# A residual added on TensorE as two rounded parts, and a bias moved from the values to the residual

## The chip, the cores and the metric

One core of one Trainium2 chip runs the whole program. The metric is the device time of one execution in microseconds (us). A core has five engines that run side by side, each with its own queue of instructions in program order: TensorE (PE; its weight loads are shown as PEld), VectorE (DVE), ScalarE (ACT), GpSimd (POOL) and SyncE (SP). They wait for each other by semaphores alone.

## The reference

x is 16 sequences of 56 tokens of 128 features. First a cross attention by autocorrelation, then a mixture of 8 experts, both added to x with a tanh gate:

```python
Q, K, V = norm(x) @ Wq + bq, ctx[:, :56] @ Wk + bk, ctx[:, :56] @ Wv + bv   # 16 heads of 8
corr = irfft(rfft(Q) * conj(rfft(K))).mean(over the 8 of a head)
w, idx = top_k(corr, 4); w = softmax(w)
out = sum_k w[k] * roll(V, -idx[k])                                        # per head
x = x + tanh(g_xattn) * (out @ Wo + bo)
logits = norm(x) @ Wr + br; weights = softmax over the 2 largest of 8
h = gelu(norm(x) @ W1[e] + b1[e]); y_e = h @ W2[e] + b2[e]                 # 128 -> 512 -> 128
x = x + tanh(g_ffn) * sum_e weights[e] * y_e
```

The weights w of a head sum to one. So the bias bv of the values comes out of the attention as bv @ Wo for every token.

## The kernel before, in words

The tokens lie in 8 tiles of 112 (two sequences each). Tiles 0 to 3 are half 0, 4 to 7 half 1, and each half has two quarters (q = 0, 1) of two tiles. `f(half, q)` in the code and in this text is the step f for that quarter. Every engine's order is written out by hand: a function for each step, waits inside it, and the calls below each other at the end of the engine's block.

The front (the attention) goes through these steps, most of them on TensorE with a copy by another engine behind each:

- keep_busy (L918): FILLERS products of a zero tile with 512 columns, before any data is there.
- context_spectra, x_spectra: discrete Fourier transform along the sequence, as a product with a table; for x on the normalised tiles xn. The results are copied to cf and xf.
- open_projection (L922) adds a bias row as a product with one row of contraction, keys, queries and values (L949, L955, L960) are the products with the weights.
- times_keys and scores on VectorE multiply the spectra, head_sums (L969) sums over a head, correlations (L981) goes back to lags, replaced and kept on VectorE find the 4 largest, exponentials on ScalarE, weights_turned (L987), weight_spectra (L991), own_columns on VectorE (L690), repeated (L997), weighted and output_spectra on VectorE (tw and of).
- output_products (L1007): of times Wo, copied with the gate to y_sb (gated, L480). add_residual (L1017) writes the residual into PSUM bank q as an f32 product with an identity of 112, and attention (L1022) adds the way back from the spectrum on top.
- xres is made on GpSimd (residual, L352): x plus the gated bias bo, in four instructions. It waits for shared (L365), which waits for the gate's tanh of ScalarE (L525).
- attended_moments and the following on VectorE, invert(1, half) on GpSimd (L336: one over the square root of the variances) and shifts(1, half) on VectorE (L620) give the second norm. VectorE and ScalarE make the normalised tiles xn, tokens_turned (L1055) transposes them into PSUM, and ScalarE and VectorE make of it a rounded lead xth (L493) and a rest xtl (L721). attended on ScalarE (L485) copies the attention's result from PSUM to x2.

The experts: all large products are made from fp32r (rounded) operands. A value is kept as a lead (rounded) and a rest (what rounding left), and a product is the sum of lead times lead, rest times lead and lead times rest. hidden(n, halves) (L1073) makes chunk n of 128 hidden features (4 chunks for each of 8 experts), ScalarE applies gelu and makes its lead, VectorE the rest (L735), project(n, halves) (L1097) is the second product. Both go over 448 tokens (a half) at a time. The weights' lead is made by ScalarE (lead, L459) for experts 0 and 1 and by GpSimd for the others, the rest by GpSimd (rest, L343, in pieces of 128 columns for experts 0 to 2, L408 whole for the others).

GpSimd's order in the front is: invert(0,0), invert(0,1), shared, residual four times, rest(0,0), rest(0,1), rest(1,0), invert(1,0), rest(1,1), lead(2,0), one piece of rest(2,0), invert(1,1), and on. Each of its instructions on this path waits for the one before it to be finished.

PSUM has 8 banks. hidden writes bank 2 * (n % 2) + half, so chunk 0 of half 0 writes bank 0, where attention(1,0) had put its result; `if n == 0 and halves == A: pe.wait_ge(x2_ok, 3)` holds it until that is copied.

Of the kernel before, what the change touches and what calls it, by code (L numbers as in the profile page):

```python
# [25 lines left out]

FILLERS = 10
SLOTS = 3
# [25 lines left out]
B_EVEN = B_ID + D  # L54
TAB_B = B_EVEN + 2

P_B2, P_B1, P_WR = 0, E, E + E * HC
# [30 lines left out]
def build(nc, first, second, w_attn, bias_rows, gates, shared_rows, cols, w_experts, tab_b, tab_c, out, route_dram):  # L88
    with ExitStack() as stack:
# [9 lines left out]
        back = sb("back", [PT, 2, HT, D])  # L99
        tb = sb("tb", [D, TAB_B])  # L100
        tc = sb("tc", [D, HT + 1, D])
        wa_sb = sb("wa_sb", [D, 4, D])
        rows_sb = sb("rows_sb", [1, 3, D])
        shared = sb("shared", [PT, D + E])
# [6 lines left out]
        tanh_g = sb("tanh_g", [D, 2])  # L111
        xres = sb("xres", [PT, NT, D])
        minus_half = sb("minus_half", [PT, HT])
        stat = sb("stat", [PT, NT, 6])
# [68 lines left out]
        c_spec, cf_ok = sem("context_spectra"), sem("context_spectra_in_sbuf")  # L183
        x_spec, xf_ok = sem("x_spectra"), sem("x_spectra_in_sbuf")
        k_proj, v_proj, q_proj = sem("k_projected"), sem("v_projected"), sem("q_projected")
# [8 lines left out]
        y_mm, y_ok, attn, x2_ok = sem("y_products"), sem("y_in_sbuf"), sem("attention_out"), sem("x2_ready")  # L194
        tanh_ok, xres_ok = sem("gates_ready"), sem("residual_with_bias")
        xt_mm, xth_ok, xt_ok = sem("x2_transposed"), sem("x2_lead"), sem("x2_split")
        wrc_mm, wrc_ok = sem("router_centred"), sem("router_centred_in_sbuf")
# [43 lines left out]
        def nth(half, q):  # L241

            return 2 * half + q + 1
# [39 lines left out]
        def banks_of(n, halves):  # L283

            return slice(2 * (n % 2) + halves[0], 2 * (n % 2) + halves[-1] + 1)

# [41 lines left out]
        def _(gp):  # L328
# [19 lines left out]
            def residual(half, q):  # L348
# [5 lines left out]
                gp.wait_ge(xres_ok, nth(half, q))  # L354

            def lead(e, k):

                gp.tensor_copy(weh[:, e, k, :], we_sb[:, e % RING, k, :]).then_inc(lead_p, 1)  # L358
                gp.wait_ge(lead_p, 2 * (e - LEAD_BY_SCALAR) + k + 1)
# [5 lines left out]
            gp.tensor_scalar(shared[:, 0:D], shared[:, 0:D], tanh_g[0:PT, 0:1], None, ALU.mult).then_inc(pool, 1)  # L365
            gp.wait_ge(pool, 1)
            residual(0, 0)
            residual(0, 1)
            residual(1, 0)
            residual(1, 1)  # L370
            gp.wait_ge(in_we[0], 16)
            gp.wait_ge(lead_s, 1)
            rest(0, 0)
            gp.wait_ge(lead_s, 2)
            rest(0, 1)
            gp.wait_ge(in_we[1], 16)
            gp.wait_ge(lead_s, 3)
# [38 lines left out]
        def _(act):  # L416
# [21 lines left out]
            def x_spectra(half, q):  # L438
                act.wait_ge(x_spec, nth(half, q))
                act.copy(xf[:, half, q * QS:(q + 1) * QS], bank[:, 2 + q, 0:QS]).then_inc(xf_ok, 1)  # L440

# [73 lines left out]
            take(kf, 0, 4)  # L515
            x_spectra(0, 0)
            x_spectra(0, 1)
            take_swapped(kf, 0, 4, 1)
            take_negated(kf, 0, 4, 1, k_ok)
            context_spectra(1)  # L520
            normalise(tokens, 0, 6)
            normalise(tokens, 0, 4)
            lead(0, 0)
            act.wait_ge(in_g, 16)
            act.activation(tanh_g[:, :], g_sb[:, :], ACT.Tanh).then_inc(tanh_ok, 1)  # L525
            act.wait_ge(k_proj, 2)
# [5 lines left out]
            exponentials(0)  # L532
            take_negated(kf, 1, 5, 1, k_ok)
            act.wait_ge(v_proj, 1)
            take(vf, 0, 0)
            lead(1, 0)
            weights_turned(0)
            take_swapped(vf, 0, 0, 0)
            act.wait_ge(v_proj, 2)
# [3 lines left out]
            take_negated(vf, 1, 1, 0, v_ok)  # L543
            head_sums(1)
            gated(0, 0)
            exponentials(1)
            gated(0, 1)
            act.wait_ge(wrc_mm, 1)
# [36 lines left out]
        def _(ve):  # L585
# [46 lines left out]
            def columns(q):  # L632
                return slice(q * QS, (q + 1) * QS)

            def times_keys(half, q):
# [150 lines left out]
            def take_expert(e, half):  # L786

                ve.wait_ge(y_expert, product_of(HC * e + HC - 1, half))
                if e >= 2:
# [5 lines left out]
                                        op0=ALU.add, op1=ALU.mult).then_inc(scaled_ok, 1)  # L795

            def turned_routes():
                ve.wait_ge(route_mm, 1)
                ve.tensor_copy(route_t[:, :], bank[0:E * NT, 5, 0:PT]).then_inc(route_sb, 1)
# [22 lines left out]
            measured_b = aggregates(second_half, measured_b)  # L822
            variances(1, measured_b)
            times_keys(0, 0)
            shifts(0, 1)
# [3 lines left out]
            normalise(tokens, 5)  # L829
            normalise(tokens, 7)  # L830
            head_sums(0)
            replaced(0)
# [81 lines left out]
        def _(pe):  # L914
# [37 lines left out]
            def queries(half, q):  # L952
                pe.wait_ge(xf_ok, nth(half, q))
                into = bank[:, 6, q * QS:(q + 1) * QS] if half else bank[:, 6 + q, 0:QS]
                pe.matmul(into, wa_sb[:, 0, :], xf[:, half, q * QS:(q + 1) * QS], start=False, stop=True,  # L955
                          skip_group_check=True).then_inc(q_proj, 1)

            def values(half):
                open_projection(2, half, HT)
                pe.matmul(bank[:, half, 0:HS], wa_sb[:, 2, :], cf[:, half, :], start=False, stop=True,  # L960
                          skip_group_check=True).then_inc(v_proj, 1)

# [48 lines left out]
            def add_residual(half, q):  # L1011

                if nth(half, q) == 1:
                    pe.wait_ge(xres_ok, 4)
                if not half:
                    pe.wait_ge(v_ok, q + 1)
                pe.matmul(bank[0:PT, q, 0:QT * D], ident[0:PT, 0:PT],  # L1017
                          xres[:, quarter(half, q), :].rearrange("p i d -> p (i d)"), start=True, stop=False)

# [38 lines left out]
            def hidden(n, halves):  # L1058
# [4 lines left out]
                if n >= 2:  # L1063
                    pe.wait_ge(gelu_ok, unit(n - 2, halves[-1]))
                if n == 0 and halves == A:
                    pe.wait_ge(x2_ok, 3)
                cols_ = slice(c * D, (c + 1) * D)
                operands = ((weh, xth), (wel, xth), (weh, xtl))
                for k, (w, t) in enumerate(operands):
                    for half in halves:  # L1070
                        if n == 0:
                            pe.wait_ge(xt_ok if k == 2 else xth_ok, half + 1)
                        mm = pe.matmul(bank[:, 2 * (n % 2) + half, 0:TOK], w[:, e, 0, cols_], t[:, half, :],  # L1073
                                       start=(k == 0), stop=(k == 2))
# [38 lines left out]
            x_spectra(0, 1)  # L1113
            context_spectra(1)
            queries(0, 0)
            queries(0, 1)
            pe.wait_ge(in_wvo, 16)
            values(0)
            keys(1)
            pe.wait_ge(in_tb, 16)  # L1120
            head_sums(0, 0)
# [3 lines left out]
            x_spectra(1, 1)  # L1125
            pe.wait_ge(qk_mul, 1)
            open_projection(0, 6, HT)
# [108 lines left out]
```

## Time and profile before

| | us |
|---|---|
| median of 3 runs | 117.72 (117.53 to 117.83) |
| the profiled execution | 117.55 |
| its span, first to last instruction | 115.7 |
| busy: TensorE, its weight loads | 110.0, 93.8 |
| busy: VectorE, ScalarE, GpSimd | 85.1, 81.6, 73.1 |

The span leaves 1.85 us around it. All durations in this text are of the one profiled execution. A matmul's duration in a timeline holds the way through the array, so rows that follow each other overlap; the chain of waits counts each stretch of time once. An f32 product shows as two matmuls, an fp32r product as one.

### The profile page before, as it was taken

To read this page: it belongs to the slowest core of one execution; us is meant where nothing else is said; L and a number is where in the kernel's file an instruction comes from. 1 tells how busy PE (TensorE), PEld (TensorE's weight loads), DVE (VectorE), ACT (ScalarE), POOL (GpSimd) and SP (SyncE) were. 2 spreads that over 40 slices of the span, in tenths; PEclk is the share of its full clock that TensorE was granted. 3 is DMA by queue.
4 is the path that set the end of the run, shared out by engine and by line. 5 is a ranking of instruction groups with operands and counts; after the bars stand their busy time and mean duration, and the time that the engine had idled before them with its cause. 6 is when DMAs were issued, how large, how long until landed. Compare 5 with 4: busy or idle time off the path is not lost.

```text
span 115.7 us, 1754 instructions
## 1 busy us (share of the span) xinstructions
PE 110.0 (95%) x577; PEld 93.8 (81%) x577; DVE 85.1 (74%) x174; ACT 81.6 (70%) x120; POOL 73.1 (63%) x74
## 2 busy tenths in 40 slices
PE   6999999999899999999999999999999999999960
PEld 2488778668578898999899999999999999999950
DVE  0473577878679998586987499769789746878891
ACT  0447986359489669978878868888778887788900
POOL 1123498813898603999999999999999702405500
PEclk9999999999999999999999999999999999999998
DMA  3989300130050050298084000400300300000004
GB/s 80 271 275 417 151 0 6 51 133 0 0 181 3 7 180 0 50 289 330 5 340 135 25 0 9 150 0 3 157 1 6 136 22 0 0 0 0 3 0 159
DMA packets 4223, 10.34 MB, mean 89 GB/s; under 512 B 837, under 2 KB 1590, under 8 KB 4214
## 3 DMA queue, kind: packets, MB, share of 16 engines
q1 hardware_dynamic: 3442, 9.65, 24.1%
q10 hardware_dynamic: 772, 0.59, 1.9%
q8 instruction: 4, 0.07, 0.2%
q14 instruction: 5, 0.04, 0.1%
HBM read 9.75 MB, written 0.49 MB: 88 GB/s over the span
## 4 chain that ended last, share of the span: by engine, by line
PE 88%; ACT 4%; DVE 3%; POOL 2%; issue 1%; DVEq 0%; POOLq 0%
PE bank L1073 34%; PE bank L1097 33%; PE bank L918 4%; PE bank L943 2%; PE bank L960 2%; PE bank L922 2%; POOL wel L343 2%; PE bank L934 2%; PE bank L955 2%; PE bank L949 2%; PE bank L969 1%; DVE kf L793 1%; PE bank L1007 1%; ACT L553 1%; PE bank L997 1%
## 5 line engine op out<-in xcount | busy, mean ns | idle before, releaser
L735 DVE TENSOR_TENSOR hidl<-prod,hidh 128x896 fp32r<-128x896 f32 (+1 forms) x37 | 47.9, 1298 | 14.1 <-ACT hidh L506 13.7
L499 ACT ACTIVATE prod<-bank,col_sb 128x896 f32<-128x896 f32 (+1 forms) x37 | 33.6, 909 | 14.2 <-PE bank L1073 12.2
L506 ACT CAST hidh<-prod 128x896 fp32r<-128x896 f32 (+1 forms) x33 | 28.9, 874 | 1.0
L397 POOL TENSOR_TENSOR cf<-cf,kf 128x448 f32<-128x448 f32 x12 | 18.8, 1584 | 11.4 <-DVE kf L793 11.3
L1073 PE MATMUL bank<-xth,weh 128*128 128x448 f32 x64 | 19.2, 368 | 0.5 <-POOL wel L343 0.4
L1097 PE MATMUL bank<-hidh,weh 128*128 128x448 f32 x64 | 19.5, 370 | 0.0
L1097 PE MATMUL bank<-hidl,weh 128*128 128x448 f32 x64 | 19.2, 366 | 0.0
L1097 PE MATMUL bank<-hidh,wel 128*128 128x448 f32 x64 | 19.1, 365 | 0.0
L1073 PE MATMUL bank<-xth,wel 128*128 128x448 f32 x64 | 19.0, 365 | 0.0
L1073 PE MATMUL bank<-xtl,weh 128*128 128x448 f32 x64 | 19.0, 365 | 0.0
L358 POOL CAST weh<-we_sb 128x512 fp32r<-128x512 f32 x12 | 14.3, 1188 | 5.8 <-issue 5.6
L408 POOL TENSOR_TENSOR wel<-we_sb,weh 128x512 fp32r<-128x512 f32 x10 | 16.0, 1604 | 0.8
L343 POOL TENSOR_TENSOR wel<-we_sb,weh 128x128 fp32r<-128x128 f32 x24 | 13.0, 542 | 3.7 <-ACT weh L459 1.9
L1073 PEld LDWEIGHTS bank<-xth,weh 128*128 128x128 f32 x64 | 12.0, 188 | 2.2 <-POOL wel L343 0.8
L1097 PEld LDWEIGHTS bank<-hidl,weh 128*128 128x128 f32 x64 | 12.0, 188 | 1.2 <-DVE hidl L735 0.2
L1097 PEld LDWEIGHTS bank<-hidh,weh 128*128 128x128 f32 x64 | 12.0, 188 | 1.2 <-POOL wel L408 0.4
L1073 PEld LDWEIGHTS bank<-xtl,weh 128*128 128x128 f32 x64 | 12.0, 188 | 1.0
L1073 PEld LDWEIGHTS bank<-xth,wel 128*128 128x128 f32 x64 | 12.0, 188 | 0.9
L1097 PEld LDWEIGHTS bank<-hidh,wel 128*128 128x128 f32 x64 | 12.0, 188 | 0.9
L336 POOL TENSOR_TENSOR rstd<-var,minus_half 112x4 f32<-112x4 f32 x4 | 4.1, 1021 | 9.6 <-DVE var L614 9.6
L793 DVE SCALAR_TENSOR_TENSOR kf<-bank,col_sb,route_b 128x448 f32<-128x448 f32 x14 | 9.4, 675 | 0.5 <-PE bank L1097 0.5
L918 PE MATMUL bank<-filler 128*128 128x512 bf16 x10 | 4.4, 629 | 1.0 <-DVE filler L801 1.0
(120 smaller groups left out, 118.4 us busy)
## 6 DMA issues: line engine op xcount, KB each, us to landing
we_sb<-in_w_experts SPq DMA_DIRECT2D x8, 512.0 KB, 3.4
route_b<-route_scratch SPq DMA_DIRECT2D x8, 448.0 KB, 3.8
out<-vf SPq DMA_DIRECT2D x2, 224.0 KB, 1.9
tc<-in_tab_c SPq DMA_DIRECT2D x1, 320.0 KB, 6.4
tb<-in_tab_b SPq DMA_DIRECT2D x1, 230.0 KB, 5.9
back<-in_second SPq DMA_DIRECT2D x1, 224.0 KB, 5.2
front<-in_first SPq DMA_DIRECT2D x1, 137.4 KB
front<-in_first ACTq DMA_DIRECT2D x1, 137.4 KB
```

The costliest lines, as they stand in the source:

```text
L336: gp.tensor_tensor(rstd[:, tiles], var[:, tiles], minus_half[:, :], ALU.pow).then_inc(rstd_ok, 1)
L343: gp.tensor_tensor(wel[:, e, k, at:at + PIECE], we_sb[:, e % RING, k, at:at + PIECE], weh[:, e, k, at:at + PIECE].bitcast(F32), ALU.subtra ...
L358: gp.tensor_copy(weh[:, e, k, :], we_sb[:, e % RING, k, :]).then_inc(lead_p, 1)
L397: gp.tensor_tensor(acc[:, half, :], acc[:, half, :], scaled[:, half, :], ALU.add).then_inc(acc_ok, 1)
L408: gp.tensor_tensor(wel[:, e, k, :], we_sb[:, e % RING, k, :], weh[:, e, k, :].bitcast(F32), ALU.subtract).then_inc(we_split, 1)
L499: act.activation(hid[:, n % 2, places(halves), :], bank[:, banks_of(n, halves), 0:TOK], ACT.Gelu, bias=col_sb[:, P_B1 + n:P_B1 + n + 1]).t ...
L506: act.copy(hidh[:, n % SLOTS, places(halves), :], hid[:, n % 2, places(halves), :]).then_inc(hid_hi_s, 1)
L735: ve.tensor_tensor(hidl[:, n % SLOTS, places(halves), :], hid[:, n % 2, places(halves), :], hidh[:, n % SLOTS, places(halves), :].bitcast( ...
L793: ve.scalar_tensor_tensor(out=into[:, half, :], in0=bank[:, 6 - 2 * (e % 2) + half, 0:TOK], scalar=col_sb[:, P_B2 + e:P_B2 + e + 1], in1=r ...
L918: pe.matmul(bank[:, into, :], filler[:, :], filler[:, 0:1].broadcast_to([D, 512]), start=True, stop=True)
L1073: mm = pe.matmul(bank[:, 2 * (n % 2) + half, 0:TOK], w[:, e, 0, cols_], t[:, half, :], start=(k == 0), stop=(k == 2))
L1097: mm = pe.matmul(bank[:, 6 - 2 * (e % 2) + half, 0:TOK], w_of(w), t[:, slot, half, :], start=(c == 0 and k == 0), stop=(c == HC - 1 and k ...
```

## The change

- Residual: ScalarE rounds xres to xresh (fp32r), GpSimd makes xresl = xres - xresh (rest_of_residual, four new instructions of 256 columns), and add_residual makes two fp32r products with a rounded identity instead of one f32 product. The identity is rounded once on ScalarE. residual(1,1) on GpSimd goes behind rest_of_residual(0,0) and (0,1); rest_of_residual(1,0) and (1,1) go behind rest(0,1) and ahead of rest(1,0), and so ahead of invert(1,0).
- Bias: values no longer opens with bv. TensorE makes bv @ Wo once (bias_of_values: bv is a new last column of the table tb), and VectorE adds it, gated, to shared (attention_bias). residual waits for that.
- Front: queries(0,0) and (0,1) go ahead of context_spectra(1) on TensorE; VectorE copies xf of half 0 in ScalarE's place; the gate's tanh goes ahead of two normalisations on ScalarE; lead(1,0) on ScalarE goes behind head_sums(1). Nine fillers instead of ten.
- Banks: hidden writes bank 2 * ((n + 1) % 2) + half, so that chunk 0 writes bank 2 and chunk 1 bank 0; the wait for x2_ok moves to chunk 1.

```diff
-FILLERS = 10
+FILLERS = 9
 SLOTS = 3
...
+            def rest_of_residual(half, q):
+
+                gp.wait_ge(xresh_ok, nth(half, q))
+                gp.tensor_tensor(xresl[:, quarter(half, q), :], xres[:, quarter(half, q), :],
+                                 xresh[:, quarter(half, q), :].bitcast(F32), ALU.subtract).then_inc(xresl_ok, 1)
+                gp.wait_ge(xresl_ok, nth(half, q))
+
             def lead(e, k):
...
             gp.wait_ge(pool, 1)
+            gp.wait_ge(bias_ok, 1)
             residual(0, 0)
...
             residual(1, 0)
+            rest_of_residual(0, 0)
+            rest_of_residual(0, 1)
             residual(1, 1)
...
             rest(0, 1)
+            rest_of_residual(1, 0)
+            rest_of_residual(1, 1)
             gp.wait_ge(in_we[1], 16)
...
                 act.wait_ge(x_spec, nth(half, q))
-                act.copy(xf[:, half, q * QS:(q + 1) * QS], bank[:, 2 + q, 0:QS]).then_inc(xf_ok, 1)
+                act.copy(xf[:, half, q * QS:(q + 1) * QS], bank[:, 2 + q, 0:QS]).then_inc(xf_ok[half], 1)
+
+            def lead_of_residual(half, q):
+
+                act.wait_ge(xres_ok, nth(half, q))
+                act.copy(xresh[:, quarter(half, q), :], xres[:, quarter(half, q), :]).then_inc(xresh_ok, 1)
...
             take(kf, 0, 4)
-            x_spectra(0, 0)
-            x_spectra(0, 1)
             take_swapped(kf, 0, 4, 1)
...
             context_spectra(1)
+            act.wait_ge(in_g, 16)
+            act.activation(tanh_g[:, :], g_sb[:, :], ACT.Tanh).then_inc(tanh_ok, 1)
             normalise(tokens, 0, 6)
             normalise(tokens, 0, 4)
+            act.wait_ge(in_tb, 16)
+            act.copy(ident_r[:, :], ident[0:PT, 0:PT]).then_inc(ident_ok, 1)
             lead(0, 0)
-            act.wait_ge(in_g, 16)
-            act.activation(tanh_g[:, :], g_sb[:, :], ACT.Tanh).then_inc(tanh_ok, 1)
             act.wait_ge(k_proj, 2)
...
             take_negated(kf, 1, 5, 1, k_ok)
+            lead_of_residual(0, 0)
             act.wait_ge(v_proj, 1)
             take(vf, 0, 0)
-            lead(1, 0)
             weights_turned(0)
+            lead_of_residual(0, 1)
             take_swapped(vf, 0, 0, 0)
...
             head_sums(1)
+            lead(1, 0)
+            lead_of_residual(1, 0)
             gated(0, 0)
             exponentials(1)
+            lead_of_residual(1, 1)
             gated(0, 1)
...
+            def x_spectra(half, q):
+
+                ve.wait_ge(x_spec, nth(half, q))
+                ve.tensor_copy(xf[:, half, columns(q)], bank[:, 2 + q, 0:QS]).then_inc(xf_ok[half], 1)
+
             def times_keys(half, q):
...
                                         op0=ALU.add, op1=ALU.mult).then_inc(scaled_ok, 1)
+
+            def attention_bias():
+
+                ve.wait_ge(bias_mm, 1)
+                ve.wait_ge(pool, 1)
+                ve.scalar_tensor_tensor(out=shared[:, 0:D], in0=bank[0:PT, 6, QT * D:3 * D], scalar=tanh_g[0:PT, 0:1],
+                                        in1=shared[:, 0:D], op0=ALU.mult, op1=ALU.add).then_inc(bias_ok, 1)
...
             variances(1, measured_b)
+            x_spectra(0, 0)
+            x_spectra(0, 1)
             times_keys(0, 0)
...
             normalise(tokens, 7)
+            attention_bias()
             head_sums(0)
...
             def queries(half, q):
-                pe.wait_ge(xf_ok, nth(half, q))
+                pe.wait_ge(xf_ok[half], q + 1)
                 into = bank[:, 6, q * QS:(q + 1) * QS] if half else bank[:, 6 + q, 0:QS]
...
             def values(half):
-                open_projection(2, half, HT)
-                pe.matmul(bank[:, half, 0:HS], wa_sb[:, 2, :], cf[:, half, :], start=False, stop=True,
-                          skip_group_check=True).then_inc(v_proj, 1)
+                pe.matmul(bank[:, half, 0:HS], wa_sb[:, 2, :], cf[:, half, :], start=True, stop=True).then_inc(v_proj, 1)
+
+            def bias_of_values():
+
+                pe.matmul(bank[0:PT, 6, QT * D:3 * D], tb[:, B_BV:B_BV + 1].broadcast_to([D, PT]), wa_sb[:, 3, :],
+                          start=True, stop=True).then_inc(bias_mm, 1)
...
                 if nth(half, q) == 1:
-                    pe.wait_ge(xres_ok, 4)
+                    pe.wait_ge(ident_ok, 1)
+                pe.wait_ge(xresl_ok, nth(half, q))
                 if not half:
                     pe.wait_ge(v_ok, q + 1)
-                pe.matmul(bank[0:PT, q, 0:QT * D], ident[0:PT, 0:PT],
-                          xres[:, quarter(half, q), :].rearrange("p i d -> p (i d)"), start=True, stop=False)
+                for part in (xresh, xresl):
+                    pe.matmul(bank[0:PT, q, 0:QT * D], ident_r[:, :], part[:, quarter(half, q), :].rearrange("p i d -> p (i d)"),
+                              start=(part is xresh), stop=False)
...
                     pe.wait_ge(gelu_ok, unit(n - 2, halves[-1]))
-                if n == 0 and halves == A:
+                if n == 1 and halves == A:
                     pe.wait_ge(x2_ok, 3)
...
                             pe.wait_ge(xt_ok if k == 2 else xth_ok, half + 1)
-                        mm = pe.matmul(bank[:, 2 * (n % 2) + half, 0:TOK], w[:, e, 0, cols_], t[:, half, :],
+                        mm = pe.matmul(bank[:, 2 * ((n + 1) % 2) + half, 0:TOK], w[:, e, 0, cols_], t[:, half, :],
                                        start=(k == 0), stop=(k == 2))
...
             x_spectra(0, 1)
-            context_spectra(1)
             queries(0, 0)
             queries(0, 1)
+            context_spectra(1)
             pe.wait_ge(in_wvo, 16)
             values(0)
+            pe.wait_ge(in_tb, 16)
+            pe.wait_ge(qk_mul, 1)
+            bias_of_values()
             keys(1)
-            pe.wait_ge(in_tb, 16)
             head_sums(0, 0)
...
             x_spectra(1, 1)
-            pe.wait_ge(qk_mul, 1)
+            pe.wait_ge(bias_ok, 1)
             open_projection(0, 6, HT)
```

## Rows read from the trace of the kernel before

**Rows 1.** The page's part 2: the clock granted to TensorE, in tenths, 40 slices.

```profile
PEclk9999999999999999999999999999999999999998
```

**Rows 2.** Busy time by stretch, 50 to 110 us: span, each engine with its count, clock, DMA.

```profile
50.00:110.00 60.00, 59.99 (x297) 55.29 (x296) 47.02 (x40) 48.67 (x52) 46.16 (x31) 1.00 0.21 75
```

**Rows 3.** The chain of waits, in order of time: start us, us, engine and line.

```profile
0.98 4.45 PE bank L918 x10
5.43 0.94 PE bank L934 x8
...
8.33 0.88 PE bank L943 x8
...
12.97 0.73 PE bank L969 x8
...
16.50 0.31 PE bank L922 x2
...
20.27 0.43 PE bank L1017 x2
...
22.24 0.69 PE bank L1007 x4
```

**Rows 4.** Timeline of GpSimd: start us, us, line, instruction, count, idle before it.

```profile
13.65 1.54 POOL L352 TENSOR_TENSOR xres<-front,shared 112x256 f32<-112x256 f32 x2
...
16.89 6.68 POOL L343 TENSOR_TENSOR wel<-we_sb,weh 128x128 fp32r<-128x128 f32 x12
26.03 1.04 POOL L336 TENSOR_TENSOR rstd<-var,minus_half 112x4 f32<-112x4 f32 x1 [2.46 <-DVE var L614]
28.99 2.06 POOL L343 TENSOR_TENSOR wel<-we_sb,weh 128x128 fp32r<-128x128 f32 x4 [1.93 <-ACT weh L459]
...
32.44 1.01 POOL L336 TENSOR_TENSOR rstd<-var,minus_half 112x4 f32<-112x4 f32 x1 [0.17 <-DVE var L614]
```

**Rows 5.** Timeline of VectorE.

```profile
10.55 0.64 DVE L630 TENSOR_TENSOR prod<-bank,kf 128x464 f32<-128x464 f32 x1 [1.77 <-PE bank L955]
...
25.71 0.17 DVE L614 TENSOR_SCALAR var<-mv 112x4 f32<-112x4 f32 x1
...
27.10 0.16 DVE L620 SCALAR_TENSOR_TENSOR shift<-mv,rstd 112x4 f32<-112x4 f32 x1 [0.23 <-POOL rstd L336]
...
27.74 0.85 DVE L625 TENSOR_SCALAR xn<-x,mv,rstd 112x128 f32<-112x128 f32 x3
...
29.86 0.62 DVE L721 TENSOR_TENSOR xtl<-bank,xth 128x448 fp32r<-128x448 f32 x1 [0.97 <-ACT xth L493]
```

**Rows 6.** Timeline of TensorE around the first hidden products.

```profile
28.69 0.58 PE L1055 MATMUL bank<-tb,xn 112*128 112x112 f32 x4
...
31.40 0.44 PE L1073 MATMUL bank<-xth,weh 128*128 128x448 f32 x1 [0.44 <-POOL wel L343]
```

**Rows 7.** Timeline of ScalarE.

```profile
8.81 0.79 ACT L440 COPY xf<-bank 128x232 f32<-128x232 f32 x2
...
15.62 0.36 ACT L454 ACTIVATE kf<-bank 128x232 f32<-128x232 f32 x1
...
16.81 0.26 ACT L476 COPY wtau_t<-bank 56x128 f32<-56x128 f32 x1
...
29.30 0.53 ACT L493 CAST xth<-bank 128x448 fp32r<-128x448 f32 x1 [0.39 <-PE bank L1055]
...
30.93 0.37 ACT L485 COPY x<-bank 112x256 f32<-112x256 f32 x1 [0.71 <-DVE stat L709]
32.29 0.64 ACT L499 ACTIVATE prod<-bank,col_sb 128x448 f32<-128x448 f32 x1 [0.99 <-PE bank L1073]
```

**Rows 8.** Timeline of TensorE's weight loads at the start.

```profile
4.90 1.28 PEld L934 LDWEIGHTS bank<-front 112*128 112x128 f32 x8 [0.38 <-DMA front<-in_first]
```

**Rows 9.** Line views of L343 and L408 (GpSimd): duration in ns, minimum, median, maximum.

```profile
L343 POOL TENSOR_TENSOR wel<-we_sb,weh x24: 455/460/1113, 16.9 to 39.1; 128x128 fp32r<-128x128 f32 x24
...
L408 POOL TENSOR_TENSOR wel<-we_sb,weh x10: 1284/1299/2167, 45.8 to 83.5; 128x512 fp32r<-128x512 f32 x10
```

More of the change, by code:

```diff
@@ L55 @@
 TAB_B = B_EVEN + 2
+B_BV = TAB_B
 P_B2, P_B1, P_WR = 0, E, E + E * HC
@@ L99, in build @@
         back = sb("back", [PT, 2, HT, D])
-        tb = sb("tb", [D, TAB_B])
+        tb = sb("tb", [D, TAB_B + 1])
         tc = sb("tc", [D, HT + 1, D])
         wa_sb = sb("wa_sb", [D, 4, D])
-        rows_sb = sb("rows_sb", [1, 3, D])
+        rows_sb = sb("rows_sb", [1, 2, D])
         shared = sb("shared", [PT, D + E])
@@ L112, in build @@
         xres = sb("xres", [PT, NT, D])
+        xresh = sb("xresh", [PT, NT, D], F32R)
+        xresl = sb("xresl", [PT, NT, D], F32R)
+        ident_r = sb("ident_r", [PT, PT], F32R)
         minus_half = sb("minus_half", [PT, HT])
@@ L183, in build @@
         c_spec, cf_ok = sem("context_spectra"), sem("context_spectra_in_sbuf")
-        x_spec, xf_ok = sem("x_spectra"), sem("x_spectra_in_sbuf")
+        x_spec, xf_ok = sem("x_spectra"), [sem("x_spectra_in_sbuf_a"), sem("x_spectra_in_sbuf_b")]
         k_proj, v_proj, q_proj = sem("k_projected"), sem("v_projected"), sem("q_projected")
@@ L195, in build @@
         tanh_ok, xres_ok = sem("gates_ready"), sem("residual_with_bias")
+        ident_ok, xresh_ok, xresl_ok = sem("identity_rounded"), sem("residual_lead"), sem("residual_split")
+        bias_mm, bias_ok = sem("bias_of_values"), sem("attention_bias")
         xt_mm, xth_ok, xt_ok = sem("x2_transposed"), sem("x2_lead"), sem("x2_split")
@@ L283, in banks_of @@
         def banks_of(n, halves):
-            return slice(2 * (n % 2) + halves[0], 2 * (n % 2) + halves[-1] + 1)
+            return slice(2 * ((n + 1) % 2) + halves[0], 2 * ((n + 1) % 2) + halves[-1] + 1)
         def add_products(engine, products, out_, done):
@@ L1216 @@
         "w_attn": _np.stack([att("Wq"), att("Wk"), att("Wv"), att("Wo")], 1),
-        "bias_rows": _np.stack([att("bq"), att("bk"), att("bv")])[None],
+        "bias_rows": _np.stack([att("bq"), att("bk")])[None],
         "gates": _np.stack([a["g_xattn"], a["g_ffn"]], 1),
@@ L1221 @@
         "w_experts": _np.concatenate([w1, w2], 2),
-        "tab_b": tab_b,
+        "tab_b": _np.concatenate([tab_b, att("bv")[:, None]], 1),
         "tab_c": tab_c,
```

## Prediction

> **What bounds the kernel now.** I read the page first. The granted clock is at full in every slice [rows 1], so no slice is explained by a throttle. The chain of waits then splits the execution. From about 33 us on it is TensorE alone, expert after expert, with 59.99 us busy of 60.00 and 0.202 us for each matmul of 448 columns [rows 2]. The change alters no operand, width or count there, so what it does must come from the first 33 us, and a shift of the first hidden products moves the end by as much.
>
> In those 33 us I followed TensorE's chain first: ten fillers, the head sums of the first half at 12.97, the residual at 20.27 [rows 3]. Until about 25 us the chain names TensorE nearly throughout, but its links are tight against other engines: at 22.24, output_products(0,1) starts when VectorE has its spectrum. Then the chain leaves TensorE. I read the timelines of GpSimd, VectorE and ScalarE for this stretch. GpSimd waits 2.46 us and starts invert(1,0) at 26.03, when VectorE's variances are there [rows 4]. VectorE's next instruction, shifts(1,0), starts at 27.10 after 0.23 idle, waiting for exactly that; behind it stand weighted(1,1), three normalisations at 27.74 and the spectrum of the last quarter [rows 5]. tokens_turned(0) starts at 28.69 when the normalised tiles are there, ScalarE copies its result at 29.30, VectorE takes the rest at 29.86 and then the moments of attention(1,0), ScalarE copies x2 at 30.93, and TensorE, idle for 0.44, starts hidden(0,A) at 31.40 [rows 5 to 7]. The view names GpSimd's wel as the releaser of that start, but by the code it waits for x2_ok 3, that ScalarE copy (30.93 + 0.37 = 31.30), because hidden(0,A) writes bank 0, where attention(1,0) lies. So this stretch is a latency chain with no slack anywhere from invert(1,0) on, and 0.44 us at its end is the price of a bank.
>
> **Fillers.** One filler is 4.45 / 10 = 0.43 us [rows 3], 512 columns, so the low level of 1.2 GHz, though the granted clock is at full. But context_spectra(0)'s weight load starts at 4.90 after waiting for the transfer of front [rows 8], and eight such loads take 1.28 together, so the first takes at least 0.16, while the fillers end at 0.98 + 4.45 = 5.43 and the chain goes on from there. With nine fillers TensorE starts at 4.90 + 0.16 = 5.06 at best, not a whole filler earlier: a gain of 0 to 0.37. I take 0.10, since a load at the low level may well take twice as long.
>
> **Queries ahead of context_spectra(1), xf copied by VectorE.** The copies leave ScalarE (0.79 for two [rows 7]) and go to VectorE, which is idle for 1.77 us before 10.55 [rows 5]. The gap is filled with two copies of 232 columns, for which I take the 0.35 to 0.40 of ScalarE's copies. TensorE now waits once for the first copy, since context_spectra(1) no longer covers it: x_spectra(0,1) lasts 0.88 / 2 = 0.44 beyond the first x_spec [rows 3], the copy and its signals take 0.5 to 0.6, so it idles 0.1 to 0.2. times_keys(0,0) comes about 0.8 us earlier, but its scores are first used by head_sums(0,0), still queued on TensorE behind context_spectra(1), values(0), the new bias product and keys(1). So the 0.8 us is not cashed.
>
> **Values' bias.** Two openings go, 0.31 us each by the one at 16.50 [rows 3]. One f32 product of 128 columns comes, 0.69 / 2 = 0.35 by output_products. Up to head_sums(0,0) the sum is -0.10 (filler) + 0.15 (copy) - 0.31 + 0.35 = +0.1 at 12.97: nothing. The wait for qk_mul ahead of the product is long met. attention_bias on VectorE (128 columns, about 0.3) lies where it was idle before rsb. The second opening, at 16.50, is gained on TensorE: values(1) and weight_spectra(0) come 0.3 earlier, but VectorE finishes times_keys(1,1) when it did, so own_columns(0) gains only about 0.15 to 0.2. That survives to invert(1,0)'s input: variances at about 25.7 instead of 25.88 [rows 5].
>
> **Residual in two parts.** One f32 product of 256 columns takes 0.43 [rows 3]. The trace has no fp32r product of that width. From below it is 256 / 448 of 0.202, 0.12; from above the full 0.20. I take 0.125, being bound by columns as those are; two of them make 0.25 instead of 0.43, 0.18 saved four times, 0.7 us of TensorE (0.1 at the dear end). It pays nothing: the first pair lies ahead of the wait at 22.24, the second in a stretch where TensorE will wait for the norms. In the Trainium skill, FP8 and Floating Point Precision, the section TensorE Precision Notes says that true FP32 takes four passes of the array; by that alone a product in two reduced parts costs half, 0.21, and the sum would be the same.
>
> **What it costs on GpSimd.** This is the term that decides. The four new rest_of_residual are two-input subtractions of 256 columns into fp32r. wel at 128 and at 512 columns took at least 455 and 1284 ns [rows 9], so 256 is 0.73 on the line between; the additions of residual at that width come every (16.89 - 13.65) / 4 = 0.81, which I take. Four are 3.24 us, against 2.46 idle before invert(1,0) [rows 4]. And the queue has new waits:
>
> - The gate's tanh moves ahead on ScalarE, but residual now waits for attention_bias: the bias product ends near 12.2, ahead of keys(1) and of head_sums at 12.97, and VectorE adds 0.3 and signals: first residual at 12.65, 1.0 earlier than 13.65. Three of them end at 15.1. A shift here doesn't enter the sum, since the next wait is later.
> - rest_of_residual(0,0) waits for ScalarE's cast, queued behind take_negated (15.62 + 0.36 = 15.98 [rows 7], bound by TensorE's and VectorE's chain and not moved). The cast is priced by x2's copy of 256 columns, 0.37: 16.35. GpSimd idles 1.3 and runs from 16.4 to 17.2.
> - rest_of_residual(0,1) waits for a cast behind take(vf,0) and weights_turned(0), the latter at 16.81 before [rows 7]: about 17.4, done 18.2. residual(1,1) done 19.0.
> - rest(0,0) and rest(0,1): eight pieces of (6.68 - 0.46) / 11 = 0.565 [rows 4], done 23.5. rest_of_residual(1,0) and (1,1): 25.15. rest(1,0), four pieces: 27.4.
>
> invert(1,0) stands behind all of it and starts at 27.4 instead of 26.03, 1.4 later (0.9 if the casts come 0.3 early and an operation costs 0.75; 1.8 if they come 0.3 late). TensorE's add_residual(1,0), which needs the rest at 24.3, is not held up. ScalarE's normalise(1,2) waits for the same norms, with gated(1,0) and lead(1,1) behind it; lead(1,1) ends near 29.9 and GpSimd's rest(1,1) starts 1.0 later than 28.99 [rows 4].
>
> **Banks.** hidden(0,A) now writes bank 2 and need not wait for x2_ok 3; hidden(1,A) does, one product later, when that copy is nearly there. This is worth the idle 0.44 [rows 6]. So the start of hidden(0,A) moves by 1.4 - 0.44 = +0.95, and the load of its first weights, which shows behind an idle TensorE, is hidden behind attention(1,1), for which I take 0.1: +0.85. gelu(0,A) at 32.29 [rows 7] moves with it, as hidden(2,A). invert(1,1) at 32.44 [rows 4] moves by about 1.2, which tokens_turned(1) just feels (under 0.1). Sum of the path: +0.8, range +0.35 to +1.3.
>
> **Rivals.** (a) GpSimd is not in the way: casts or subtractions come so much faster that invert(1,0) keeps to its variances. Then it starts at 25.8, 0.2 earlier, and the bank gives 0.44: -0.65, 116.9. For it speaks only that 2.46 us stood idle there; against it the 3.24 + 1.3 us placed before. It decides from invert(1,0) before 26.5 (0.44 late): earlier is faster, later is slower. (b) Delay and bank cancel: invert(1,0) between 26.1 and 26.8, time 117.2 to 117.9. It needs two of the waits of GpSimd to be overestimated. (c) The bank gives nothing, since hidden(0,A) then waits for another thing as late (xtl of VectorE, also shifted): +1.4, 119.0. Against: xtl would be ready at 31.9, TensorE reaches the third product after 32.5. (d) TensorE's clock: the fillers run at the low level, the eight products at 5.43 at the high one. If the chip rises later for one filler less, or falls in the new idle of some 1.8 us between logits(0) and tokens_turned(0), products run at 1.2 GHz for a stretch; 3 us of work at the low level costs 1.5, 119.9. In the trace idle stretches of 0.44 brought no fall, and longer ones aren't in it. TensorE: Matmul & The Clock Gate in the Trainium skill, Part 1, says that idling sends the clock to half until activity has gone on for a while, and that the start of its window is not tied to the kernel; by that one filler less could matter in some executions only.
>
> **How the numbers follow.** The profiled execution took 117.55 (span 115.7 and 1.85 around it); 117.55 + 0.8 = 118.35. The median of the runs is 0.17 above that execution, so I say 118.4, with 117.9 to 118.9 for this case alone. Chances: forecast 0.62, (a) 0.14, (b) 0.12, (c) 0.08, (d) 0.04. 0.3% is 0.35 us, about what this measurement can tell from no change. Faster is (a) and a little of (b), 0.16; same is the rest of (b) and the forecast's low edge, 0.12; slower 0.72. The range from 117.3 to 119.1 leaves out (a), (d) and the top of (c).
>
> **What would show it.** invert(1,0) on GpSimd at 27.4 with no idle before it; VectorE idle 1.5 to 2 us before shifts(1,0); rest_of_residual near 0.73 each, a wait of about 1.3 before the first; TensorE idle before tokens_turned(0), which starts near 30.0; hidden(0,A) near 32.2 right behind attention(1,1); head_sums(0,0) still near 13.0. The prediction is wrong if GpSimd waits for variances there, or if the steady stage has another length than before.

## The result and the profile after

| | before | after |
|---|---|---|
| median (lowest to highest) | 117.76 (117.53 to 117.83), 4 runs | 120.46 (120.02 to 120.94), 4 runs |
| ratio, 95% interval | | 1.0241 (1.0202 to 1.0281) |
| the profiled execution, its span | 117.55, 115.7 | 120.45, 118.7 |

The change makes the kernel 2.4% slower, by 2.7 us. It was forecast slower, at 118.4 with 119.1 as the upper end, so the size was missed. An execution more than 1.5% above the fastest of its kernel is left out of the ratios in this text and kept in the medians.

The timeline of GpSimd after the change answers to [rows 4]:

```profile
13.51 1.54 POOL L358 TENSOR_TENSOR xres<-front,shared 112x256 f32<-112x256 f32 x2 [0.60 <-POOL shared L378]
...
16.57 0.73 POOL L365 TENSOR_TENSOR xresl<-xres,xresh 112x256 fp32r<-112x256 f32 x1 [0.71 <-ACT xresh L463]
17.47 0.78 POOL L365 TENSOR_TENSOR xresl<-xres,xresh 112x256 fp32r<-112x256 f32 x1 [0.17 <-ACT xresh L463]
18.32 0.73 POOL L358 TENSOR_TENSOR xres<-back,shared 112x256 f32<-112x256 f32 x1
19.13 4.34 POOL L349 TENSOR_TENSOR wel<-we_sb,weh 128x128 fp32r<-128x128 f32 x8
23.55 1.53 POOL L365 TENSOR_TENSOR xresl<-xres,xresh 112x256 fp32r<-112x256 f32 x2
25.16 2.10 POOL L349 TENSOR_TENSOR wel<-we_sb,weh 128x128 fp32r<-128x128 f32 x4
27.33 1.04 POOL L342 TENSOR_TENSOR rstd<-var,minus_half 112x4 f32<-112x4 f32 x1
```

The reader is to see that the last row, invert(1,0), has no idle in brackets: GpSimd comes to it from its queue, 1.30 later than before, while the variances were there. VectorE shows the other side, and TensorE what came of it (VectorE's row answers to [rows 5], TensorE's to [rows 6]):

```profile
28.40 0.16 DVE L647 SCALAR_TENSOR_TENSOR shift<-mv,rstd 112x4 f32<-112x4 f32 x1 [1.46 <-POOL rstd L342]
```

```profile
29.99 0.98 PE L1102 MATMUL bank<-tb,xn 112*128 112x112 f32 x4 [1.44 <-DVE xn L652]
```

So far this is the forecast. But the four transposes take 0.98 us where they took 0.58. Busy time by stretch of one microsecond (PE, PEld, DVE, ACT, POOL, then the granted clock) says why:

```profile
28.00:29.00 1.00, 0.55 (x6) 0.46 (x5) 0.60 (x2) 0.40 (x1) 0.37 (x1) 1.00 0.00 0
29.00:30.00 1.00, 0.01 (x1) 0.04 (x1) 1.00 (x5) 0.96 (x3) 0.00 (x0) 0.80 0.00 0
30.00:31.00 1.00, 1.00 (x6) 1.00 (x7) 0.20 (x1) 0.00 (x0) 0.88 (x2) 0.50 0.00 0
31.00:32.00 1.00, 1.00 (x5) 0.94 (x5) 0.42 (x1) 0.66 (x2) 0.84 (x3) 0.50 0.00 0
32.00:33.00 1.00, 1.00 (x4) 0.48 (x3) 0.47 (x3) 0.35 (x1) 0.85 (x3) 0.50 0.00 0
33.00:34.00 1.00, 1.00 (x6) 0.89 (x5) 0.93 (x7) 0.37 (x1) 0.33 (x1) 1.00 0.61 197
```

TensorE idles from about 28.55 on, the clock falls from 2.4 to 1.2 GHz at 29.6, while it idles, and all it does from 30 to 33 is at half speed. In the kernel before the granted clock was at full from the start to the last products [rows 1]. The chain of waits, TensorE's way after the norms and the first and last pieces of the expert stage (42 pieces from 60.35 on, the last a double one):

```profile
27.33 1.05 POOL rstd L342
...
29.99 0.98 PE bank L1102 x4
30.97 0.86 PE bank L1052 x4
31.84 1.53 PE bank L1069 x4
33.37 0.64 PE bank L1120 x3
...
57.67 1.21 PE bank L1120 x6
58.88 1.47 PE bank L1144 x6
60.35 1.24 PE bank L1120 x6
...
111.19 2.50 PE bank L1144 x12
```

The second thing to see is 1.24: six matmuls of 448 columns took 1.21 to 1.22 up to 57.67, like before the change, and 1.24 from 60.35 to the end, at a granted clock of full:

```profile
50.00:110.00 60.00, 60.00 (x292) 54.37 (x291) 45.06 (x39) 47.45 (x50) 45.54 (x32) 1.00 0.23 79
```

292 matmuls against 297 in the same 60 us [rows 2].

The 3.0 us between the two spans go like this. hidden(2,A) starts at 34.72 instead of 32.98: 1.74, the late norms and the low clock together. The stall at project(12) starts at 58.88 where before it was at 56.99, so 0.15 more is lost between. From there to the last products the stage takes 0.98 longer (before it ran from 58.45 to 108.31, 49.86 us; now from 60.35 to 111.19, 50.84). The remaining 0.1 is in the last steps.

### The profile page after: what moved, and what is told of

It reads as the page before. It is cut to its first block, busy times and chain, and to the rows that moved or that the text cites. A ratio compares the mean times of both kernels' runs of the same rounds, so it can differ in the third digit from the quotient of the medians.

```text
span 118.7 us, 1764 instructions
## 1 busy us (share of the span) xinstructions
PE 111.5 (94%) x574; PEld 94.5 (80%) x574; DVE 85.6 (72%) x177; ACT 82.2 (69%) x123; POOL 75.1 (63%) x78
## 4 chain that ended last, share of the span: by engine, by line
PE 82%; POOL 8%; DVE 3%; ACT 2%; issue 2%; POOLq 0%; DVEq 0%
PE bank L1120 33%; PE bank L1144 33%; POOL wel L349 5%; PE bank L960 3%; PE bank L976 2%; POOL xresl L365 2%; PE bank L991 1%; PE bank L985 1%; PE bank L1102 1%; PE bank L1069 1%; DVE kf L825 1%; PE bank L997 1%; POOL rstd L342 1%; PE bank L964 1%; PE bank L1052 1%
## 5 line engine op out<-in xcount | busy, mean ns | idle before, releaser
L767 DVE TENSOR_TENSOR hidl<-prod,hidh 128x896 fp32r<-128x896 f32 (+1 forms) x37 | 46.8, 1268 | 15.8 <-ACT hidh L529 15.6
L371 POOL CAST weh<-we_sb 128x512 fp32r<-128x512 f32 x12 | 13.4, 1113 | 5.4 <-issue 5.2
```

What stands on the lines that cost most here:

```text
L767: ve.tensor_tensor(hidl[:, n % SLOTS, places(halves), :], hid[:, n % 2, places(halves), :], hidh[:, n % SLOTS, places(halves), :].bitcast( ...
```

## The experiments

Times below are medians with the ratio to the kernel before on the same chip. That kernel's own median was 117.56, 118.41 and 118.05 in the three groups of runs, with single executions from 116.85 to 119.85 and one of 124.97, so ratios say more than times.

Every execution, profiled or not, also has its mean granted clock on record. One stretch of 3.4 us at 1.2 GHz brings it to between 0.980 and 0.986, one twice as long to 0.965 to 0.971, and without such a stretch it is 0.992 to 1.000. By that figure the clock fell in all four executions of the changed kernel (0.984, 0.985, 0.969, 0.984).

**Which part is late, and what it costs.** The first group was run together.

invert(1,0) ahead of rest(1,0) on GpSimd:

```diff
             rest_of_residual(1, 1)
+            invert(1, 0)
             gp.wait_ge(in_we[1], 16)
...
             rest(1, 0)
-            invert(1, 0)
```

> The changed kernel with invert(1,0) moved ahead of the four pieces of rest(1,0) on GpSimd, nothing else. If the delay of invert(1,0) behind the new subtractions is the cause, it starts at about 25.8 when its variances are there, TensorE's idle of 1.44 us before tokens_turned(0) goes, the granted clock doesn't fall, hidden(0,A) starts near 30.8, and the time is 116.9 if the expert stage runs at 1.22 us for six matmuls. If the clock falls or the stage stays at 1.24 us for another reason (one filler less, the table's new column), the time is 118 to 119.5 though invert(1,0) is early.

Measured: 117.44, ratio 0.9994 (0.9966 to 1.0022). The clock stays at full (by its mean in nine of the ten executions), invert(1,0) starts at 26.23 after waiting for its variances. The whole loss is gone, with the new subtractions, the new front, nine fillers and the bias all in place. The gain of 0.65 that was expected on top isn't there, and VectorE's timeline shows one reason:

```profile
27.30 0.41 DVE L647 SCALAR_TENSOR_TENSOR shift<-mv,rstd 112x4 f32<-112x4 f32 x1 [0.23 <-POOL rstd L342]
27.64 0.62 DVE L657 TENSOR_TENSOR tw<-bank,vf 128x464 f32<-128x464 f32 x1
28.19 0.98 DVE L652 TENSOR_SCALAR xn<-x,mv,rstd 112x128 f32<-112x128 f32 x3
```

GpSimd now runs rest(1,0) beside these, and the first and third take 0.41 and 0.98 instead of 0.16 and 0.85.

Ten fillers instead of nine in the changed kernel:

```diff
-FILLERS = 9
+FILLERS = 10
```

> The changed kernel with ten fillers again. If the fall of the clock comes from the idle before tokens_turned(0), it stays and the time is 120.0 to 121.0. If one filler less let the clock fall, the fall goes and the time is near 118.4.

Measured: 119.94, ratio 1.0233 (1.0164 to 1.0302). The clock falls all the same, in the profiled execution for twice as long (at 1.2 GHz from 29.0 to 35.8 us). By the mean clock it fell in all four executions. In the three others the stretch was of the usual length once (0.986) and about twice as long twice (0.969 and 0.971), and the three took 119.92 to 119.94 all the same. The filler is not the cause.

Six filler products in TensorE's idle, into bank 2, which is free from then on:

```diff
             logits(0)
+            pe.wait_ge(of_mul, 3)
+            keep_busy(6, 2)
             tokens_turned(0)
```

> The changed kernel with six more filler products of 512 columns (0.21 us each at the high level, 1.3 us) on TensorE between logits(0) and tokens_turned(0), where it idled for 1.44 us. invert(1,0) stays at 27.3. If that idle makes the clock fall, the clock now stays at full, the front part gains about 0.9 to 1.0, and the time is 119.5 with the expert stage at 1.24 us for six matmuls, 118.4 with 1.22. If the fall has another cause the time stays at 120.5.

Measured: 118.75, ratio 1.0072 (1.0031 to 1.0112). invert(1,0) is as late as in the changed kernel (27.09), but the granted clock stays at full, in this profile and by the mean in all ten executions (0.993 to 1.000). Its timeline of TensorE, and two of its stretches:

```profile
28.37 1.25 PE L960 MATMUL bank<-filler 128*128 128x512 bf16 x5
29.75 0.58 PE L1102 MATMUL bank<-tb,xn 112*128 112x112 f32 x4
```

```profile
29.00:30.00 1.00, 0.87 (x6) 0.38 (x5) 0.96 (x4) 0.72 (x2) 0.20 (x1) 1.00 0.00 0
30.00:31.00 1.00, 1.00 (x10) 0.79 (x8) 0.07 (x1) 0.64 (x2) 0.84 (x3) 1.00 0.00 0
```

Five of the six fillers have a record. The transposes are back at 0.58, and hidden(2,A) starts at 33.35: 0.37 after that of before, or 0.6 if one allows for a front that runs 0.24 earlier in this execution. That is the cost of the delay less the gain of the bank, which the forecast had at 0.8; by the ratio it is 0.85 (0.4 to 1.3). hidden(2,A) of the changed kernel starts at 34.72, so the low clock costs 1.1 to 1.4 us by the traces. The ratio falls from 1.0241 (1.0171 in a repetition, below) to 1.0072, which is 1.0 to 1.7%, 1.2 to 2.0 us. Either way it comes out dearer than the delay that led to it. The profiled execution of this kernel has the expert stage at 1.24 too, without any fall of the clock.

The f32 residual in the changed kernel:

```diff
-            rest_of_residual(0, 0)
-            rest_of_residual(0, 1)
...
-                for part in (xresh, xresl):
+                pe.matmul(bank[0:PT, q, 0:QT * D], ident[0:PT, 0:PT], xres...)
```

> The changed kernel with the residual as one f32 product again: no rounding on ScalarE, no subtractions on GpSimd; bias, order of the front, nine fillers and banks as changed. If the two parts of the residual are what costs, invert(1,0) waits for its variances at about 25.8 and the time is 116.9 to 117.1. If the cost comes from bias, order or fillers, it stays above 118.5.

Measured: 117.22, ratio 0.9980 (0.9941 to 1.0019). GpSimd idles 3.00 before invert(1,0) at 26.07, hidden(0,A) starts at 30.65. The two parts are the cost.

**The same from the other side.** The kernel before with the banks swapped and nothing else:

```diff
-                if n == 0 and halves == A:
+                if n == 1 and halves == A:
...
-    mm = pe.matmul(bank[:, 2 * (n % 2) + half, 0:TOK], ...
+    mm = pe.matmul(bank[:, 2 * ((n + 1) % 2) + half, 0:TOK], ...
```

> The kernel before with the banks of hidden swapped and the wait for x2_ok moved to chunk 1, nothing else. If the bank is worth the idle of 0.44 ahead of hidden(0,A), that product starts at about 30.95 instead of 31.40 and the time falls by 0.4 to 0.5, to about 117.1. If something else holds hidden(0,A) as long, no change.

Measured: 117.72, ratio 0.9952 (0.9908 to 0.9996). tokens_turned(0) starts at 28.89 and hidden(0,A) at 30.81, and hidden(2,A) at 32.51, 3.62 behind tokens_turned(0), where it was 32.98 - 28.69 = 4.29. By the ratio the gain is 0.56 us (0.05 to 1.1), against the 0.44 that were worked out.

The kernel before with invert(1,0) delayed by work that nobody needs. The added instructions write a spare tile and leave the output as it is:

```diff
+            for i in range(7):
+                gp.tensor_tensor(spare[:, :], xres[:, 0, :], xres[:, 1, :],
+                                 ALU.subtract).then_inc(spare_ok, 1)
+                gp.wait_ge(spare_ok, i + 1)
             rest(1, 0)
             invert(1, 0)
```

> The kernel before with seven idle-handed subtractions of 128 columns on GpSimd ahead of rest(1,0), into a tile that nobody reads, and nothing else changed: ten fillers, old front, f32 residual. If the late invert(1,0) is enough for all that was measured, it starts near 27.4, TensorE idles over 1 us before tokens_turned(0), the granted clock falls and the time is 120 to 121.3 (0.4 more than the changed kernel, as the bank isn't swapped). If the loss needs the new front or the two parts too, the time stays below 119.2 (1.4 later and nothing more) and the clock doesn't fall.

Measured: 119.93, ratio 1.0126 (1.0061 to 1.0191). invert(1,0) starts at 27.14, TensorE waits for it, and the clock falls here too, later than in the changed kernel. From its timeline of TensorE and its stretches:

```profile
29.80 0.57 PE L1061 MATMUL bank<-tb,xn 112*128 112x112 f32 x4 [1.43 <-DVE xn L631]
```

```profile
30.00:31.00 1.00, 1.00 (x10) 0.84 (x8) 0.03 (x2) 0.59 (x2) 0.84 (x3) 1.00 0.00 0
31.00:32.00 1.00, 0.87 (x4) 0.32 (x2) 1.00 (x3) 0.33 (x1) 0.85 (x3) 0.78 0.00 0
32.00:33.00 1.00, 0.94 (x3) 0.50 (x2) 0.75 (x5) 0.37 (x1) 0.92 (x2) 0.50 0.09 33
```

So a late invert(1,0) alone, in the old kernel, brings the wait, and in this execution the fall. The cost is smaller than expected: 1.0126 is 1.5 us, where 2.5 to 3.5 were expected and the changed kernel had 2.0 to 2.8. By the mean clock it fell in only two of the four executions (0.980 twice, at 119.90 and 119.95); the other two (0.997 and 1.000) took 120.00 and 118.70. So half the executions paid for the delay alone. Whether the rest of the difference comes from the later start of the fall, when the transposes are done, isn't shown.

The residual in two parts alone, on the kernel before. The edit is the residual's part of the change; with it lead(1,0) on ScalarE goes behind head_sums(1), which is one of the moves of the front:

> The kernel before with the residual in two parts and nothing else (bias, front, ten fillers and banks as before; xresl lies in memory of expert 7's weights, which are made later). If the two parts on GpSimd are the whole cost, invert(1,0) starts at 27.0 to 27.5, the clock falls and the time is 0.3 to 0.5 above the changed kernel, whose bank swap is missing here: 120.3 to 121. If bias or front carry a part of the cost, it is below the changed kernel.

Measured: 119.78, ratio 1.0152 (1.0089 to 1.0215), beside the changed kernel's 1.0171 in the same group. The profiled execution, the longest of the four (121.60), has invert(1,0) at 27.78 and the low clock from 30.7 to 34.1:

```profile
27.78 1.07 POOL L340 TENSOR_TENSOR rstd<-var,minus_half 112x4 f32<-112x4 f32 x1
```

Its front was 0.66 late from the first products on (the first opening started at 6.96, before at 6.30), TensorE idled 0.91 ahead of tokens_turned(0), and the clock fell all the same. But the ratio is of the other three executions, and their mean clock was 1.000: no fall, and still 1.5%, 1.8 us. That is the late invert(1,0) with neither the fall nor the bank. The 0.3 to 0.5 more than the changed kernel isn't seen; the intervals are too wide for it, and most of the changed kernel's executions had the fall. Bias, order of the front and fillers carry no part of the cost that could be measured. Whether they carry a gain was asked by a second run of the f32 residual beside the banks alone, in one group:

> The changed kernel with the f32 residual, a second time and beside the banks alone. If bias, front and fillers are worth nothing besides the bank, it equals the banks alone within 0.2 us, at about 117.1 to 117.3. If they gain 0.1 to 0.3 of their own, it is lower by that.

Measured: 118.11, ratio 0.9953 (0.9906 to 1.0000), against 0.9952 for the banks alone. No gain is seen; with intervals of half a per cent to each side, 0.1 to 0.3 us could not be told from none.

**The interval of 1.24.** In the changed kernel it began behind the stall at project(12). GpSimd's wait for route_ok taken out of the changed kernel:

```diff
             rest(2, 1)
-            gp.wait_ge(route_ok, 1)
```

> The changed kernel without GpSimd's wait for route_ok ahead of expert 3's weights (no race guards it), so that these are ready early and TensorE doesn't stall at project(12). The fall of the clock at 30 us stays. If that stall tips the expert stage from 1.22 to 1.24 us for six matmuls, the stage stays at 1.22 and the time is 119.0 to 119.4. If the 1.24 comes from something else, such as the fallen clock, it stays and the time is 120.2 (the stall's 0.25 less).

Measured: 128.51, ratio 1.0738 (1.0635 to 1.0842): neither theory had this. GpSimd starts expert 3's weights at 41.40, in the changed kernel at 47.00, while VectorE works through the routing, in many short instructions. VectorE's and GpSimd's timelines (the profiled execution is the longest of the four, 130.48):

```profile
45.17 1.29 DVE L796 TENSOR_SCALAR lden<-ltanh 112x64 f32<-112x64 f32 x1
...
48.97 1.31 DVE L804 TENSOR_TENSOR lexp<-lexp,lmask 112x64 f32<-112x64 f32 x1
```

```profile
44.85 1.56 POOL L425 TENSOR_TENSOR wel<-we_sb,weh 128x512 fp32r<-128x512 f32 x1
...
48.94 1.26 POOL L425 TENSOR_TENSOR wel<-we_sb,weh 128x512 fp32r<-128x512 f32 x1
```

lden took 0.20 and lexp 0.23 when GpSimd stood still. Here they end at 46.46 and 50.28, and GpSimd's end at 46.41 and 50.20: these short instructions of VectorE wait for the long one of GpSimd to be done. lmask does too (0.99 instead of 0.16, to 48.38 beside 48.30); the reciprocal between them keeps its time (0.54, undisturbed 0.55). TensorE waited up to 3.90 us for a hidl behind them, and its clock fell a second time. The stall at project(12) never came, and the stage ran at 1.24 from 60.45 on, so 1.24 comes without the stall. It comes without the fall too (the filled gap), and a fall doesn't bring it (the late invert(1,0) alone ran at 1.22).

Two more profiles of kernels already seen tell more about it. The changed kernel again:

> The changed kernel as it is, a second time beside the kernel before. If the fall of the clock is a consequence of the idle, it shows again near 29 to 31 us and hidden(2,A) starts 1.5 to 2.5 later than before. The interval for six matmuls in the expert stage is 1.24 us again if it belongs to this kernel, 1.22 in some executions if it is a matter of chance; the time is 119.5 to 121.

Measured: 119.81, ratio 1.0171 (1.0118 to 1.0224). Its chain of waits, the profiled execution (120.05):

```profile
59.51 1.45 PE bank L1144 x6
60.96 1.22 PE bank L1120 x6
62.18 1.21 PE bank L1144 x6
```

1.22 behind the same stall, to the end. The clock fell again (0.73 granted in the stretch from 30 to 31, 0.50 in the next two).

The kernel before again:

> The kernel before as it is, one more profile. If 1.22 us for six matmuls in the expert stage belongs to this kernel, it shows again all through and the time is 117.2 to 117.8. If it is a matter of chance, a stretch with 1.24 shows and the time is up to 1.2 longer.

Measured: 117.40, one execution. Its chain of waits:

```profile
45.93 1.24 PE bank L1073 x6
...
55.85 1.24 PE bank L1073 x6
57.09 1.23 PE bank L1097 x6
58.32 1.21 PE bank L1073 x6
```

Nine pieces in a row at 1.24 and then 1.21 to 1.22 to the end, with the change of interval at turn_routes and at project(12). So both intervals come in both kernels. A stage that stays at 1.24 costs 1.0 us, and the changed kernel's first profile had that, the second not. All of before's first profile was at 1.22. It may well come more often with the change: of the seven profiled executions with a late invert(1,0) five had it to the end (all but the changed kernel's second and the late invert(1,0) alone), of the seven with an early one none, two for a stretch. That it hangs on the late invert(1,0), and by what, isn't shown, so a part of the 2.7 us may be this and not the fall. What sets it stays open.

**Can the two parts be kept?** invert(1,0) early, and GpSimd held until VectorE's normalisations are done:

```diff
             rest_of_residual(1, 1)
+            invert(1, 0)
+            gp.wait_ge(xn_v, 8)
...
-            invert(1, 0)
...
-            rest(1, 1)
+            rest(1, 1, 0)
+            rest(1, 1, 1)
+            invert(1, 1)
+            rest(1, 1, 2)
+            rest(1, 1, 3)
...
-            invert(1, 1)
```

> The changed kernel with invert(1,0) ahead of rest(1,0) on GpSimd, and rest(1,0) held until VectorE's first three normalisations of the attended tokens are done; invert(1,1) goes into the middle of rest(1,1). With invert(1,0) early alone, VectorE's shift took 0.41 instead of 0.16 and the normalisations 0.98 instead of 0.85 while GpSimd worked beside them. If that nearness cost the rest of the gain, hidden(0,A) now starts at 30.6 to 30.8 and the time is that of the f32 residual with the new banks, 0.3 to 0.5 under the kernel before. If not, it equals the kernel before.

Measured: 117.77, ratio 0.9989 (0.9957 to 1.0021). VectorE's timeline has its old durations back:

```profile
27.37 0.16 DVE L651 SCALAR_TENSOR_TENSOR shift<-mv,rstd 112x4 f32<-112x4 f32 x1 [0.23 <-POOL rstd L342]
...
28.00 0.85 DVE L656 TENSOR_SCALAR xn<-x,mv,rstd 112x128 f32<-112x128 f32 x3
```

hidden(0,A) starts at 30.87, with the banks alone at 30.81. But the work of GpSimd that was held back now ends at 43.0, with the banks alone at 39.7, and so lies beside the routing on VectorE: lden takes 0.45 and lexp 0.48, and TensorE idles 0.31 at 44.17 for a hidl. Of the bank's 0.44 those 0.31 are given back there. No order of GpSimd's work that was tried beats the one without the subtractions.

## Why the prediction was wrong

Right, by its own steps:

- invert(1,0) at 27.4: measured 27.33, with no idle before it. The four subtractions took 0.73 to 0.78, forecast 0.73, and two in a row came 0.8 apart, where the sum had 0.81.
- VectorE idle 1.46 before shifts(1,0) (1.5 to 2 forecast), tokens_turned(0) at 29.99 (30.0), head_sums(0,0) at 13.12 (13.0).
- The bank: 0.56 by the ratio, against 0.44. Bias and front: nothing that could be measured at the end, as summed. The filler's 0.10 wasn't there: context_spectra(0) started 0.42 earlier (5.01 instead of 5.43) but took 1.45 instead of 0.94. That time differs between kernels with ten fillers too (1.59 in the parts alone), so it isn't shown to be the missing filler's.
- The fp32r products of 256 columns come 0.12 apart in the two pairs that follow each other (26.25, 26.37, 26.49), forecast 0.125. A pair by itself saves nothing: from 20.23 to 20.64, 0.41 where one f32 product had 0.43 [rows 3]. It paid nothing, as said.
- The delay less the bank: 0.4 to 0.6 by the trace of the filled gap and 0.85 by its ratio, forecast 0.8.

Inside the way to 27.4 two terms erred and cancelled. attention_bias waited for shared, done only at 12.9, so the first residual started at 13.51, not 12.65. The wait for ScalarE's first cast was 0.71 and not 1.3, since its end was given by the cast as said (16.57 against 16.4).

Wrong: the step that took TensorE's idle for free. The text saw "the new idle of some 1.8 us between logits(0) and tokens_turned(0)", named the fall of the clock as rival (d) and gave it 0.04, because 0.44 of idle had brought no fall. It brought one in all six profiled executions that had 0.9 us or more of idle there, and none where it was 0.42 or less or filled. hidden(0,A), forecast near 32.2, started at 33.02. The cost, 1.1 to 1.4 us by the traces and 1.2 to 2.0 by the ratios of the filled gap, is the term that was missing from the sum; rival (d) had it at 1.5 us and was right but for its chance. That the fall and not the idle is the dear part rests on the filled gap. Executions of one kernel don't price it closer: in the changed kernel's repetition the one without a fall (0.999) took 119.11, the five with one 118.99 to 120.51.

The Trainium skill, TensorE: Matmul & The Clock Gate, Part 1, says that idling sends the clock to half rate and that activity brings it back, and the trace agrees. By that page of the Trainium skill, though, an idle as short as this one would not be enough; 1.44 us were, and 0.91 in one execution, so the measurement decides. The same page of the Trainium skill also says that the start of its window isn't tied to the kernel, and the trace agrees: the low stretch began at 29.6 in one execution of the changed kernel and at 30.5 in another, 1.0 and 1.6 after the idle began.

The fall is no certainty either. By the mean clock it came in 13 of the 14 executions of the changed kernel with nine or ten fillers, in two of four of the late invert(1,0) alone and in one of four of the parts alone. With an early invert(1,0) some 120 executions show it eight times, and no profile shows where. What makes the changed kernel fall more often than the two others isn't shown.

Not foreseen at all: that 448 columns can come at two intervals, 0.203 and 0.207. The prediction named a steady stage of another length as a sign of being wrong, and that sign came: 50.84 us instead of 49.86. Without the slower interval the first profile would have been 1.0 shorter; in the second the stage was 49.86 again. A small slip is in the forecast itself: 118.35 and 0.17 make 118.5, not 118.4.

## What to carry to other kernels

An idle of TensorE is not only its own length: behind 1.44 us of it came 3.4 us at half clock, in most executions, which cost more than the delay. Where a change opens a gap that can't be closed, a few products into a free bank can hold the clock. Here they took no time of their own: tokens_turned(0) started at 29.75 with them and at 29.74 in the kernel with ten fillers.

Work that moves from TensorE to another engine is paid in that engine's queue. Look for the short instruction behind it that a latency chain needs (here the inverse root of four columns), and put that first.

## What the runs showed of the hardware

- Behind 1.44 us of idle the clock was at 1.2 GHz for 3.4 us, with the fall already within the idle in one execution of the changed kernel (0.80 granted from 29 to 30), 0.1 us after TensorE had gone on in another, and 1.8 us after in the kernel with the late invert(1,0) alone (0.78 from 31 to 32). In the one with ten fillers it lasted twice as long. In other executions of the same kernels it didn't come at all.
- A short instruction of VectorE can take as long as the GpSimd instruction beside it: 1.29 and 1.31 us instead of 0.20 and 0.23. The Trainium skill, GPSIMD Engine Reference, Key points, says that the two share their interfaces to SBUF and contend when VectorE is in a mode with two ports or has two SBUF inputs; lexp has two inputs, and the trace agrees. lden has one, and the trace doesn't show which mode it was in.
- Six fp32r products of 448 columns take 1.215 or 1.24 us at a granted clock of full, for tens of microseconds. They change from one to the other mostly at turn_routes or at project(12), with or without a stall there.
